# A graph network's last dense rows: twelve of 49 steps in the second mean aggregation, 37 in the projection

## The reference, cut to what matters

```python
# third layer: two mean aggregations, the second of which gives its output
h   = relu(mean_of_edges(x)  @ W1l.T + b1 + x @ W1r.T)
out =      mean_of_edges(h)  @ W2l.T + b2 + h @ W2r.T
x   = layernorm(x + out)
# fourth layer: attention over the edges
Q, K  = x @ qw, x @ kw                   # 4 heads of 32
alpha = (Q[src] * K[dst]).sum(-1) / sqrt(32)
a     = softmax of alpha over the edges of one dst
agg   = segment_sum(Q[src] * a, dst)
h     = layernorm(agg) * gamma + beta
x     = layernorm(x + silu(h) @ out_w + out_b)
```

## Time and profile before

| | |
|---|---|
| median of 3 runs | 2851.87 us (2850.75 to 2859.87) |
| the profiled execution | 2858.08 us, its span 2856.4 us |
| DVE busy | 2304.9 us, 81% of the span |
| PE, ACT, POOL busy | 1829.5, 1742.4, 1697.1 us |

### The profile page before, as it was taken

One profiled execution on the slowest core, in us unless ns is written; L12 is line 12 of the kernel. 1 busy time (PEld: TensorE's weight loads), 2 busy tenths in 40 slices (PEclk: granted clock), 3 DMA queues, 4 the chain that ended last, 5 costly groups with the idle time before them and its releaser, 6 DMA issues. The chain is left out here.

```text
span 2856.4 us, 51702 instructions
## 1 busy us (share of the span) xinstructions
PE 1829.5 (64%) x9687; PEld 1364.1 (48%) x9687; DVE 2304.9 (81%) x9111; ACT 1742.4 (61%) x4459; POOL 1697.1 (59%) x1605
## 2 busy tenths in 40 slices
PE   5667666566666546777777666657675666557763
PEld 4556555444444424545554333335564555534442
DVE  7987887998888857788877688858886999888882
ACT  3545545332223226878777688855555888868885
POOL 7777777266666663333332666637775776327675
PEclk8777777788888877999889889989997888766776
DMA  6777787444444447999998789967886988734441
GB/s 201 245 243 247 239 253 229 144 82 76 79 79 79 79 76 274 330 343 341 334 325 321 249 294 301 301 206 252 262 259 206 301 292 289 268 130 167 153 160 52
DMA packets 280171, 625.34 MB, mean 219 GB/s; under 512 B 51230, under 2 KB 84649, under 8 KB 280055
## 3 DMA queue, kind: packets, MB, share of 16 engines
q1 hardware_dynamic: 207543, 523.73, 53.7%
q0 software_dynamic: 72512, 100.52, 16.0%
HBM read 342.76 MB, written 285.23 MB: 220 GB/s over the span
## 5 line engine op out<-in xcount | busy, mean ns | idle before, releaser
L1258 ACT ACTIVATE node_out<-node_in,n_shift,n_root 128x128 f32<-128x128 f32 (+1 forms) x1176 | 468.1, 482 | 81.7 <-DVE n_shift L1579 81.6
L791 POOL DMA_INDIRECT sums<-gat_sums,dst_safe_i x196 | 185.2, 945 | 305.4 <-DVE pre L2008 255.8
L912 POOL DMA_INDIRECT out_dram<-node_x2t,out_index x196 | 209.2, 1067 | 158.0 <-ACT node_x2t L1466 95.9
L799 POOL DMA_INDIRECT src_rows<-x_table,row_i x200 | 202.2, 1011 | 128.8 <-issue 53.8
L799 POOL DMA_INDIRECT sums<-x_table,row_i x192 | 192.9, 1005 | 87.0 <-issue 50.3
L799 POOL DMA_INDIRECT own_rows<-in_x_dram,dst_safe_i x196 | 191.7, 978 | 59.7 <-issue 59.7
L858 POOL DMA_INDIRECT gat_sums<-src_rows,add_idx x100 | 160.2, 1602 | 112.5 <-DMA gat_sums<-sums,add_idx 31.4
L1562 DVE BATCH_NORM_STATS2 n_stats<-node_in 128x6 f32<-128x256 f32 (+1 forms) x588 | 209.3, 419 | 21.3 <-DMA node_in<-y_nodes 10.5
L1267 ACT ACTIVATE t_a<-ps 128x512 f32<-128x512 f32 (+1 forms) x198 | 115.8, 585 | 166.6 <-PE ps L957 166.4
L858 POOL DMA_INDIRECT gat_sums<-sums,add_idx x96 | 154.0, 1604 | 91.0 <-issue 33.1
L1267 ACT ACTIVATE t_b<-ps 128x512 f32<-128x512 f32 (+1 forms) x198 | 115.9, 586 | 96.5 <-PE ps L957 96.4
(11 more groups left out here) (420 smaller groups left out, 6563.3 us busy)
## 6 DMA issues: line engine op xcount, KB each, us to landing
own_rows<-x_table SPq DMA_DIRECT2D x245, 256.0 KB, 3.0
node_in<-in_x_dram SPq DMA_DIRECT2D x96, 512.0 KB
x_table<-node_out SPq DMA_DIRECT2D x96, 512.0 KB
x_table<-new_rows SPq DMA_DIRECT2D x147, 256.0 KB
gat_sums<-node_x2t SPq DMA_DIRECT2D x49, 528.0 KB
acc_dump<-acc SPq DMA_DIRECT2D x98, 264.0 KB
node_sums<-gat_sums SPq DMA_DIRECT2D x48, 528.0 KB
h_table<-node_h SPq DMA_DIRECT2D x48, 512.0 KB, 4.9
```

Of the source, the lines that this page charges most:

```text
L791: g_.indirect_dma_start(out=to[:, g.b, j, 0:width], out_offset=None, in_=tab, in_offset=bass.IndirectOffsetOnAxis(ap=indices(j), axis=0)). ...
L799: g_.indirect_dma_start(out=to4[g.q][:, j, 0:F], out_offset=None, in_=tab, in_offset=bass.IndirectOffsetOnAxis(ap=indices(j), axis=0)).the ...
L912: g_.indirect_dma_start(out=out[:, :], out_offset=bass.IndirectOffsetOnAxis(ap=out_index[:, t:t + 1], axis=0), in_=wide_new[:, g.b, j, :], ...
L1258: last = sc.activation(to[0:pn, g.b, j, :], rows[0:pn, g.b, j, 0:F], ACT.Identity, bias=NORM[k][2][0:pn, g.b, j:j + 1], scale=root[0:pn, j ...
```

## The change

The dense steps 0 to 11 move to the second mean aggregation, one in four of its steps (`Spaced`): they use the one buffer 0 of `node_in` and `node_out`, are loaded in the queue of step 4n (`load_last_nodes`), added to in step 4n+1, measured in 4n+2 (root in the same step), inverted in 4n+3, and their eight tiles are written in two halves, in 4n+3 and 4n+4; the store stands in step 4n+4. The steps 12 to 48 stay in the projection, in three of four of its steps (`Packed`), with three buffers (`node_y` is the third). The own rows of the projection get four buffers (own_rows and own2_rows) instead of two. SP's wait for the stores of the third layer's dense rows moves from the head of the projection to that of the second mean aggregation. In the second layer three semaphores become one that counts three parts; its instructions stay. Cut:

```diff
+SPACED = 12
...
+class Spaced(Step):
+    def __init__(self, g):
+        super().__init__(g.of4, 0, g.q, g.of4)
+    def index(self):
+        return self.of4
+class Packed(Step):
+    def __init__(self, g):
+        super().__init__(g.of4, g.q, g.q, g.of4)
+    def index(self):
+        return 3 * self.of4 + (self.q + SPACED)
+class Thirds:
+    def __init__(self, ring, third):
+        full = (DENSE_FULL - SPACED) // 3
+        self.sems, self.first = [*ring.sems, third], ring.base[0]
+        self.base = [ring.base[0] + 16 * SPACED, ring.base[1], 0]
+        self.end = [self.base[0] + 16 * (full + len(TAIL_PARTS)), self.base[1] + 16 * full, 16 * full]
+def wait_third_landed(eng, t, g):
+    if is_tail(g):
+        eng.wait_ge(t.sems[0], t.end[0])
+    else:
+        eng.wait_ge(t.sems[g.b], 16 * g.of4 + ((t.first if isinstance(g, Spaced) else t.base[g.b]) + 16))
+def wait_third_drained(eng, t, g):
+    base = t.first if isinstance(g, Spaced) else t.base[g.b]
+    if base or not (isinstance(g.of4, int) and g.of4 == 0):
+        eng.wait_ge(t.sems[g.b], 16 * g.of4 + base)
+def wait_third_free(eng, signal, g):
+    if isinstance(g, Spaced):
+        eng.wait_ge(signal.sem, g.index() + signal.base)
+    elif isinstance(g.of4, int) and g.of4 == 0:
+        eng.wait_ge(signal.sem, signal.base + SPACED)
+    else:
+        eng.wait_ge(signal.sem, g.index() + (signal.base - 2))
+def spaced(lag, stage):
+    def turn(g):
+        if g.q == 0 and not (isinstance(g.of4, int) and g.of4 >= SPACED):
+            stage(Spaced(g))
+    return (lag, turn, STEPS)
+def packed(lag, stage):
+    def turn(g):
+        if g.q < 3:
+            stage(Packed(g))
+    return (lag, turn, STEPS)
...
+        own_in4 = Quad([*flow["att1"]["own"].sems, *flow["sage2"]["own2"].sems],
+                       [*flow["att1"]["own"].base, *flow["sage2"]["own2"].end], 1, STEPS)
+        flow["att2"]["own"] = Ring(own_in4.sems[0:2], own_in4.end[0:2], 1, WIDE_STEPS)
...
+            def load_last_nodes(g):
+                D = flow["nodes4"]
+                wait_third_free(sp, D["n_row"], g)
+                for lo, hi in parts(g):
+                    sp.dma_start(in3[g.b][lo:hi, :, :], node_rows(x3_table, SLOTS, g)[lo:hi]).then_inc(rows_in3.sems[g.b], 16)
...
-            pipeline(sp, STEPS, edges((0, both), (1, dump), (4, store)))
+            pipeline(sp, STEPS, edges((0, both)) + [spaced(0, load_last_nodes)] + edges((1, dump), (4, store)) + [spaced(4, store_last_nodes)], per=4)
...
+            def load_own4(g):
+                wait_free4(sp, L["spread"], g)
+                sp.dma_start(own4[g.q], slot_rows(x3_table, back(g))).then_inc(own_in4.sems[g.q], 16)
...
-            pipeline(sp, DENSE_FULL, edges((0, load_own_back(L, x3_table, own_rows))) + [nodes(0, load_nodes(D, x3_table, SLOTS, "n_row"))]
-                     + edges((2, store_q)) + [nodes(2, store_nodes(D, out, 0))])
+            pipeline(sp, DENSE_FULL, edges((0, load_own4)) + [packed(1, load_last_nodes)]
+                     + edges((3, store_q)) + [packed(3, store_last_nodes)], per=4)
...
+            def last_node_rows(lo, hi):
+                def make(g):
+                    D, pn = flow["nodes4"], dense_p(g)
+                    if lo == 0:
+                        wait_third_drained(act, rows_out3, g)
+                        wait_done(act, D["n_nm"], g)
+                    for j in range(lo, hi):
+                        last = sc.activation(out3[g.b][0:pn, j, :], in3[g.b][0:pn, j, :], ACT.Identity,
+                                             bias=shift3[g.b][0:pn, j:j + 1], scale=root3[g.b][0:pn, j:j + 1])
+                    if hi == DJ:
+                        last.then_inc(D["n_row"].sem, 1)
+                return make
...
-            pipeline(act, STEPS, edges((3, new_x3), (2, root), (0, sage_copies)))
+            pipeline(act, STEPS, edges((3, new_x3), (2, root)) + [spaced(2, last_node_root)] + edges((0, sage_copies))
+                     + [spaced(3, last_node_rows(0, J)), spaced(4, last_node_rows(J, DJ))], per=4)
...
-            pipeline(act, DENSE_FULL, [nodes(1, roots(D, "n")), nodes(1, normed_rows(D, "n", node_in, node_out, "n_row", "n_out"))]
-                     + edges((1, queries_keys_out), (0, att_copies)))
+            pipeline(act, DENSE_FULL, [packed(1, last_node_root), packed(1, last_node_rows(0, DJ))]
+                     + edges((1, queries_keys_out), (0, att_copies)), per=4)
...
+            def last_more(g):
+                D, pn = flow["nodes4"], dense_p(g)
+                wait_third_landed(dve, rows_in3, g)
+                v.tensor_tensor(in3[g.b][0:pn, :, :], in3[g.b][0:pn, :, :],
+                                local3_bc[0:pn, None, :].to_broadcast([pn, DJ, F]), ALU.add).then_inc(D["n_pre"].sem, 1)
+            def last_moments(g):
+                D, pn = flow["nodes4"], dense_p(g)
+                wait_done(dve, D["n_pre"], g)
+                wait_third_free(dve, D["n_row"], g)
+                for j in range(0, DJ, 2):
+                    made = v.bn_stats(stats3[g.b][0:pn, j:j + 2, :].rearrange("p j c -> p (j c)"),
+                                      in3[g.b][0:pn, j:j + 2, :].rearrange("p j f -> p f j"))
+                made.then_inc(D["n_bn"].sem, 1)
+                wait_done(dve, D["n_bn"], g)
+                v.tensor_scalar(root3[g.b][0:pn, :], stats3[g.b][0:pn, :, 2], 1.0 / F, EPS, ALU.mult, ALU.add).then_inc(D["n_ve"].sem, 1)
...
-            pipeline(dve, STEPS, edges((3, x3_shifts), (0, sources_landed), run[0], (2, x3_sums), run[1], (2, x3_moments), run[2], run[3],
-                                       (0, means)), per=4)
+            pipeline(dve, STEPS, edges((3, x3_shifts)) + [spaced(3, last_inverses), spaced(3, last_shifts)]
+                     + edges((0, sources_landed), run[0], (2, x3_sums), run[1], (2, x3_moments), run[2], run[3], (0, means))
+                     + [spaced(1, last_more), spaced(2, last_moments)], per=4)
...
-            pipeline(dve, DENSE_FULL, edges(spread[0]) + [nodes(1, node_inverses)] + edges(spread[1]) + [nodes(1, node_shifts)]
-                     + edges(spread[2], (2, products), spread[3], (2, score_sums)) + [nodes(0, nodes_x3_more), nodes(0, nodes_x3_moments)])
+            pipeline(dve, DENSE_FULL, edges(spread[0]) + [packed(1, last_inverses)] + edges(spread[1]) + [packed(1, last_shifts)]
+                     + edges(spread[2], (2, products), spread[3], (2, score_sums)) + [packed(0, last_more), packed(0, last_moments)], per=4)
```

More of the change, by code:

```diff
@@ L511, in gnn_program @@
         WIDE_FIX, WIDE_LAST_B = Step(WIDE_STEPS // 2, WIDE_STEPS % 2), (WIDE_STEPS - 1) % 2
+        in3, out3 = ([ring[:, 0, :, :], ring[:, 1, :, :], node_y[:, i, :, :]] for i, ring in enumerate((node_in, node_out)))
+        stats3, root3, shift3 = ([NORM["n"][i][:, 0], NORM["n"][i][:, 1], NORM["a"][i][:, 0]] for i in range(3))
         own4 = [rows[:, b, :, :] for rows in (own_rows, own2_rows) for b in range(2)]
@@ L604, in load_nodes, with store_last_nodes @@
                 return load
+            def load_last_nodes(g):
[3 more added lines that the diff above has]
+                    sp.dma_start(in3[g.b][lo:hi, :, :], node_rows(x3_table, SLOTS, g)[lo:hi]).then_inc(rows_in3.sems[g.b], 16)
+            def store_last_nodes(g):
+                wait_done(sp, flow["nodes4"]["n_row"], g)
+                for lo, hi in parts(g):
+                    sp.dma_start(node_rows(out, 0, g)[lo:hi], out3[g.b][lo:hi, :, :]).then_inc(rows_out3.sems[g.b], 16)
             def store_nodes(D, tab, base):
@@ L707, in _ @@
             wait_all(sp, flow["sage1"]["stored"])
+            wait_all(sp, flow["nodes3"]["n_out"])
             sp.wait_ge(fix_out_sem, 16 * 2)
@@ L904, in _ @@
             L = flow["att2"]
-            wait_all(pool, flow["nodes4"]["n_out"])
+            for b in range(3):
+                pool.wait_ge(rows_out3.sems[b], rows_out3.end[b])
             def scatter_rows(g):
@@ L1261, in normed_rows, with last_node_root @@
                 return make
+            def last_node_root(g):
+                D, at = flow["nodes4"], root3[g.b][0:dense_p(g), :]
+                wait_done(act, D["n_ve"], g)
+                sc.activation(at, at, ACT.Sqrt).then_inc(D["n_rt"].sem, 1)
+            def last_node_rows(lo, hi):
[10 more added lines that the diff above has]
+                return make
             def copy_out(L, g, bank, to, produced, copied, free, jn=J):
@@ L1444, in _ @@
             L = flow["att2"]
-            wait_all(act, flow["nodes4"]["n_out"])
+            for b in range(3):
+                act.wait_ge(rows_out3.sems[b], rows_out3.end[b])
             def silu(g, jn=WJ):
@@ L1849, in add @@
                     if i == 0:
-                        wait_landed(dve, L["own"], g)
+                        wait_quad(dve, own_in4, g)
                         wait_free(dve, L[used], g)
@@ L1858, in add @@
```

(3 more changed lines are left out.)

47 lines of the change are left out of this document (19 added, 28 removed).

## The result

The changed kernel takes **2953.52 us** (median of 4 runs, 2946.11 to 2962.97) against 2855.87 of the kernel before in the same comparison (4 runs, 2850.75 to 2872.33): a ratio of **1.033**, with a 95% interval of 1.0302 to 1.0359. The prediction was 2939 us, in a range of 2885 to 2975, slower with 0.89. The profiled execution is longer by 2951.0 - 2856.4 = 94.6 us.

A forecast was written before the change was run, and what follows sets the result against it. The prediction took DVE to set the pace in the projection and nearly so in the second mean aggregation, where dumps in SP's queue release its steps. 86 + 39 - 38 = +87 on 2851.87 gave 2939 us, range 2885 to 2975.

The forecast's parts named there:

- Term 1: Second mean aggregation: eleven dumps held back by SP's wait for n_row, 7.8 us each, +86 us (75 to 93).
- 3.48 + 1.0: Stalled step: 3.48 us from the dump's issue to the running sum, plus 1.0 for the 512 KB in front.
- the 5.79 of the earlier trace: First mean aggregation: 5.79 us from a 512 KB load's issue to its reader, giving 1.68 as upper end.
- Term 2: Second mean aggregation: DVE's part of the twelve moved dense steps, 3.3 us each, +39 us (30 to 44).
- The 3.67: Projection: DVE's time for one dense step, inverse and shift included, 3.67 us, carried to the second mean aggregation.
- Term 3: Projection: time got back with one dense step of four less, -38 us (-44 to -19).
- POOL's 5.40: Projection: POOL as the next bound, four gathers with the gaps between them taking 5.40 us per step.
- DVE's pace of 5.41: Projection: DVE's time per step once one dense step of four is gone, 5.41 us; alone a gain of 44.
- The rest at nothing: Extra buffers, ACT's eight tiles, SP's earlier wait for old stores and the single semaphore: counted as 0 us.
- 1: Second mean aggregation: SP's wait is free because n_row comes before SP asks; 2853 us, chance 0.07.
- rival 2: Second mean aggregation: SP's wait is free and DVE's gaps take up the 3.67; -38, 2814 us, chance 0.05.
- Rival 3: Second mean aggregation: behind the late dump the next own-row load comes late; 44 us more, 2983 us, chance 0.10.

The follow-up runs named there:

- thin transfers: Changed kernel with the moved dense steps' loads and stores cut from 512 KB to 64 KB: ratio 1.0232 to the kernel before.
- load last: Changed kernel with SP issuing the dense load and store behind the step's dump and store: ratio 1.0256 to the kernel before.
- both: Changed kernel with all eight tiles written one step earlier on ACT, and SP's dense load and store behind dump and store: ratio 1.0143 to the kernel before.
- tiles around: Changed kernel with four tiles ahead of ACT's copies and four behind in one step, dense load last in SP's queue: ratio 1.0093 to the kernel before.
- own buffers alone: Kernel before with only four buffers for the projection's own rows and its loops unrolled by four: ratio 0.9995 to the kernel before.
- around, lag: As tiles around, with the dense store one step later and the projection's later stages lagging one step more: ratio 1.003 to the kernel before.

## Why the prediction was right, by its steps

- **Term 1, +86: it measured (13.09 - 5.09) x 11 = 88.** The chain is the one worked out. Counted from the running sum at 2053.55, t_b ends at 6.28 (predicted 6.08), the tiles at 7.81 (7.73), the load goes at 8.01 (7.76), the dump at 8.66 (8.39), the sum at 13.08 (12.87). From dump to sum 3.48 + 1.0 was said and 4.45 came, so the 1.0 taken for the 512 KB in front measured 0.97. That it fits so well is luck, since thin transfers and load last show that the reasoning around it was loose: the 3.48 already held about 1.0 that the dump alone doesn't take, and the 5.79 of the earlier trace rows isn't the price of a 512 KB load here (in "load last" one released its reader 4.34 after its issue, 4.16 to 4.46 in eleven rounds). The Trainium skill (DMA: Bandwidth & Descriptors, Queues, rings and completion order) says that an SDMA engine takes up descriptors in the order of its ring and that a semaphore's increment lands only after all earlier writes of that engine. By that rule and the 5.79 I had worked out 1.68, and with 4.34 the same working gives 4.34 - 0.63 - 3.48 = 0.23. The trace has neither. That the dump lands sooner behind fewer bytes (2.44 against 4.45) agrees with it in direction; whether it waits for the whole load no row shows, since none tells when the load landed in these steps.
- **Term 2, +39: it measured 32.** The three steps behind take 5.97 + 6.73 + 5.22 = 17.92 against 15.27, 2.65 x 12. The size was off by 7. The 3.67 was elapsed time of the projection, gaps included (the two long instructions are 2.63 of its 3.31); here the two steps take 1.07 and 1.83 more than the 4.90 of a step without wait, 2.90 together. The five kinds of dense instructions are busy for 1.22, 1.41, 0.17, 0.20 and 0.17 in the round of 2053.55, together 3.17, so some 0.3 of it lies in gaps that DVE has anyway. In every version the second and third steps take 5.97 to 6.00 and 6.71 to 6.73, except where late data hold them up (load last, both, tiles around): no order tried here removed this part.
- **Term 3, -38: it measured -24.5, the largest miss**, within its bounds of -44 to -19 (the five other kernels with this projection give -29 to -19). The projection ran at 274.5/48 = 5.72 per step, not at 5.4 to 5.6. The step that failed is POOL's 5.40: "the two will get in each other's way now and then". POOL became the bound outright: 195 gathers behind the first, in 275.4 us, are 1.412 each, 5.65 for four, without a wait. In the kernel before there were 24.4 us of waits for PE in POOL's 288.9, and 288.9 - 24.4 = 264.5 would have been left if a gather had stayed as short. That it got longer, 1.12 instead of 1.07 in the middle of the stretch, cost the remaining 11. DVE's pace of 5.41 wasn't reached; in the step of four without dense work, and in the one behind it, it also waited for ACT. Waits of DVE after, 2345 to 2575:

```profile
DVE n_root L2264 <- ACT n_root L1365: 9.4, 9, 1.8
DVE pre L2297 <- ACT gate L1552: 8.8, 10, 1.3
```

- **The rest at nothing** holds: own buffers alone measured 0.9995. The eight tiles on ACT are covered, apart from their place in the chain, in the changed kernel; in "both" they were not.
- 88 + 32 - 24.5 = 95.5, against 94.6 of the span and a forecast of 87: two more from term 1, seven less from term 2, and 13.5 from the smaller return of the projection. That this closes to a microsecond is partly chance. The last step's first running sum moved by 115.5 (2158.0 to 2273.5), not by 88 + 32 = 120; the first score follows it 4.3 later than before (41.5 instead of 37.2), and this makes up the rest.
- **Rivals.** 1 and 2 needed SP's wait to be short: it was 6.4. Even with that wait nearly gone (around, lag) the second and third steps stay at 5.97 and 6.73, so rival 2's second condition, gaps of DVE that take up the 3.67, fails by itself. Rival 3, the late load of own rows, isn't there: the interval behind the stall is 5.97, DVE's own work, and that load goes out 1.8 us behind the dump (2064.01, L742).

Why a gather takes longer the two traces show, though no run was made for it. Three lines of the projection of the changed kernel, where L2247 is the dense step's addition and L896 the gather:

```profile
2348.77 1.22 DVE L2247 TENSOR_TENSOR node_in<-node_in,local_bc 128x1024 f32<-128x1024 f32 x1
2349.10 1.71 POOL L896 DMA_INDIRECT sums<-x_table,row_i  x1 [0.30 <-issue]
...
2351.11 0.95 POOL L896 DMA_INDIRECT sums<-x_table,row_i  x1 [0.30 <-issue]
```

The gather that starts inside the addition ends 0.82 after it; the next one takes 0.95. Of the 196 gathers there, 36 start inside such an addition and 34 inside the products (L2297, an instruction of the same kind), and every one of them ends 0.80 to 0.83 after that instruction, or takes its usual 0.94 where that is more. All 62 gathers of more than 1.1 us are among these. In the kernel before it is the same with 38 and 20, to within 0.03 (an addition hits a gather with 0.58 us still to run there, and with 0.80 after, on average). Together these cost POOL 31.2 us beyond the 0.945 of an undisturbed gather after, and 22.7 before: 8.4 of the 9.5 by which the gathers' sum grew (208.2 to 217.7). So POOL's price was no constant to begin with, and once POOL goes from gather to gather without a wait, its gathers start earlier in DVE's additions. What of the two instructions gets in the other's way no row shows.

## What to carry to other kernels

A wait in a queue that issues in order belongs to everything behind it: before a transfer is put into such a queue, look at what stands behind it, and whether the thing it waits for comes later in the same step than that. Idle time of an engine in a stretch is room only if it lies where the moved work can go; here the step without any wait (4.90 of 5.09) told more than the 35 us of the window. When work leaves a stretch, the return ends at the next engine, and that engine's pace has to be taken with a margin, since its instructions may slow down as well: here a gather's price depended on when it started beside DVE.

## What the runs showed of the hardware

- The time from the issue of the same store, the dump of 264 KB, to the start of its reader differs with what goes out around it. It was 2.44 us with a 64 KB load 0.65 ahead and a 64 KB store 1.2 behind, and 4.45 with 512 KB each (means over the eleven stalls of thin transfers and of the changed kernel). It was 3.48 with a 256 KB load 0.63 ahead (one step). Where a load and a store of 512 KB each went out some 4.0 and 3.5 ahead, with loads of own rows in between, it was 5.30 ("both") and 6.46 ("tiles around", means over eleven rounds). What the load ahead and what the store behind adds was not told apart.
- The same gather on POOL has its shortest time everywhere alike (0.94), but its mean moves with the stretch: 961 ns in the second mean aggregation, 1064 in the projection before, 1103 and 1145 for its two forms after (2345 to 2575). In both projections the longer ones are those that start inside an addition or a multiplication of two f32 tensors on DVE: they end 0.80 to 0.83 us after it. Gathers that start inside DVE's moments (L2255) or score sums (L2301) take 0.94 to 0.95 in the changed kernel.
